# Sums of squares of the query and key heads gathered into 32-row strips, one root and reciprocal for four chunks

## The chip, the cores and the metric

One NeuronCore of a Trainium2 chip runs the whole program. The engines named below are TensorE (PE; PEld is its weight load), VectorE (DVE), ScalarE (ACT), GpSimd (POOL) and SyncE (SP), which here only issues DMAs (transfers between the on-chip memory SBUF and the large memory HBM). Matrix products land in PSUM, eight banks of 128 partitions x 512 fp32 numbers; POOL cannot read PSUM. The metric is the time of one execution on the device in microseconds, the median of several runs.

## The reference

Three layers follow each other on x of shape (4, 1024, 256), all in fp32: half a feed-forward step, an attention step, and half a feed-forward step again.

```python
x = L0_attn_x
x = x + 0.5 * ffn(layernorm(x))
x = x + attn(layernorm(x))
x = x + 0.5 * ffn(layernorm(x))
```

In the attention step, 16 heads of 64 columns each, the part that matters here is the projection and the l2 norm of q and k:

```python
def l2norm(t, eps=1e-12):
    return t / jnp.clip(jnp.linalg.norm(t, axis=-1, keepdims=True), eps)
q = (x @ Wq).reshape(b, n, H, DH).transpose(0, 2, 1, 3)
k = (x @ Wk).reshape(b, n, H, DH).transpose(0, 2, 1, 3)
v = (x @ Wv).reshape(b, n, H, DH).transpose(0, 2, 1, 3)
...
q = l2norm(q)
k = l2norm(k)
dots = jnp.einsum('bhid,bhjd->bhij', q, k) * QK_SCALE
```

After it come a mixing of the heads, a causal mask, the 64 largest scores of each row, a softmax, a second mixing, the product with v, a sigmoid gate and the output projection.

## The kernel before

The program has three stages with a barrier between them: `first_stage` (the first feed-forward layer, and the projections q, k, v and the gates, all stored to HBM), `attention`, and `last_stage`. Only `first_stage` is touched. It loops over M = 8 blocks m of MACRO = 512 tokens.

The order on each engine is written out by hand; the engines meet at semaphores (`s["name"]`), and nothing is rescheduled. For one block TensorE does: `heads(m)`, the 16 chunks c of q and k (128 columns, that is two heads, each), with the values and the turning of the next block's normed x put between; `up(m+1)` and `down(m+1)`, the next block's feed-forward; and `gates(m)`. A chunk has two products of 128x128 by 512 tokens (L314). Head columns lie on the partitions and tokens in the columns, so the sum over a head's 64 columns is a sum over partitions.

A chunk c of q or k goes through these steps before:

- PE L314 makes the chunk in PSUM bank c % 4.
- ACT squares it into `sq` (L431) and copies it to `copy` (L434). These buffers and `rt`, `rr`, `ri`, `qn`, `vo` are parts of tile `a_share` in the profile (copy is `a_copy`).
- PE L323 multiplies `sq` with `blocks` (128x128, 1 where row and column are of one head). Bank 4 + c % 2 then holds the sum of squares of each head, repeated on its 64 partitions.
- ACT takes the root into `rt` (L440), POOL its maximum with 1e-12 into `rr` (L529), DVE the reciprocal into `ri` (L585).
- POOL multiplies `copy` and `ri` into `qn` (L537), and SP stores two chunks at a time (L240).

So root, maximum and reciprocal each work on 128 x 512 numbers per chunk, of which only 2 x 512 differ.

The values (L330), the turned blocks (L277) and the gates (L341) go through banks 6 and 7 in turn, in the order of `side_uses`. In the last block (m = 7) there is no further feed-forward: `early_scores` (L354, L355) makes some scores for the attention between the gates, and DVE takes over the gates' scaling from POOL (`last_gates`, L602). `first_stage` ends when SP has seen the last store land.

Of the kernel before, what the change touches and what calls it, by code (L numbers as in the profile page):

```python
# [25 lines left out]
QC = 2 * HP  # L26
VC = TT * (INNER // 512)
# [32 lines left out]
def build(nc, x, Wq, Wk, Wv, mix_rows, mem_kT, mem_v, hs_col, Wg, bg_col, Wo, WfcT, lnw_col, lnb_col, WpT,  # L60
          ident_c, blocks_c, delta_c, mask_c, guess_c, out):
# [11 lines left out]
    with ExitStack() as top:  # L73
# [7 lines left out]
        with ExitStack() as ctx:  # L81
            ffn_w = ctx.enter_context(nc.sbuf_tensor("ffn_w1", [P, FFN_W], F32))
            first_stage(nc, (banks, ps, ident, ffn_w, eps), x, x1d, Wq, Wk, Wv, Wg, bg_col, hs_col, mem_kT, mkT, qd, kd, vd, gd,
                        wd, ident_c, blocks_c, WfcT, WpT, lnw_col, lnb_col, sd)
# [16 lines left out]
def side_uses():  # L101

    order = []
    for m in range(-1, M):
# [10 lines left out]
        if m >= 0:  # L115
# [4 lines left out]
FIRST_STAGE_SEMS = dict(k0_in=1, q0_in=1, k0=1, s_ps=1, s_sb=1, s_st=1, c_in=6, asum=1, tot=1, wfc=1, tern=1, wp=1, sums=1, done=1, ones=1, kept=1, w_in=7, memk=1, mem=1, x_in=2, link=1, xna=1, xnb=1, side=1, side_out=1, hid=1, gelu=1, sq=1,  # L120
                      stat=1, std=1, hstat=1, hstd=1, gsum=1, out=1, res=1, stored=2, proj=1, raw=1, inv=1, square=1, ssq=1, norm=1,
                      clip=1, qk=1, qk_st=2, v_st=2,
# [3 lines left out]
def first_stage(nc, consts, x, x1d, Wq_d, Wk_d, Wv_d, Wg_d, bg_col, hs_col, mem_kT, mkT, qd, kd, vd, gd, wd, ident_c,  # L126
                blocks_c, WfcT, WpT, lnw_col, lnb_col, sd):
# [4 lines left out]
    with ExitStack() as ctx:  # L132
        def sb(name, shape):
# [26 lines left out]
        copy = sb("copy", [P, 4, MACRO])  # L160
# [4 lines left out]
        blocks = sb("blocks", [P, P])  # L165
        ones = sb("ones", [P, P])
# [15 lines left out]
        sq, rt, rr, ri = [share[:, 2, k * WN // 2:(k + 1) * WN // 2].rearrange("p (k n) -> p k n", k=2)  # L182
                          for k in range(4)]
# [8 lines left out]
        def _(sp):  # L192
# [16 lines left out]
            sp.dma_start(blocks[:], blocks_c).then_inc(s["c_in"][5], 16)  # L209
            sp.dma_start(mraw[:], mem_kT).then_inc(s["w_in"][0], 16)  # L210
# [16 lines left out]
            for m in range(M):  # L227
# [9 lines left out]
                for p in range(HP):  # L237
                    sp.wait_ge(s["qk"], m * QC + 2 * p + 2)
                    c = 2 * p % HP
                    sp.dma_start((qd if 2 * p < HP else kd)[b, :, c:c + 2, tok],  # L240
                                 qn[:, p % 2]).then_inc(s["qk_st"][p % 2], 16)
                    if p == 1 and m + 2 < M:
# [3 lines left out]
                    if p % 2 == 1:  # L246
                        t = p // 2
                        sp.wait_ge(s["side_out"], SIDE["v", m, 2 * t + 1] + 1)
                        sp.dma_start(vd[b, tok][t * P:(t + 1) * P, :], vo[:, t % 2]).then_inc(s["v_st"][t % 2], 16)
# [14 lines left out]
        def _(pe):  # L264
# [15 lines left out]
            def up(m):  # L280
                pe.wait_ge(s["side_out"], SIDE["ta", m, 1] + 1)
                for h in range(FC):
                    if h >= 2:
                        pe.wait_ge(s["gelu"], m * FC + h - 1)
                    elif m >= 1:
                        pe.wait_ge(s["norm"], m * QC - 1 + h)
# [17 lines left out]

            def heads(m):
                pe.wait_ge(s["side_out"], SIDE["tb", m, 1] + 1)
                for c in range(QC + 1):
                    if c < QC:
                        if c >= 4:
                            pe.wait_ge(s["raw"], m * QC + c - 3)  # L310
                        else:
                            pe.wait_ge(s["res"], m * TT + c + 1)
# [4 lines left out]
                    if c >= 1:  # L317
                        pe.wait_ge(s["square"], m * QC + c)
                        if c >= 3:
                            pe.wait_ge(s["norm"], m * QC + c - 2)  # L320
                        else:
                            pe.wait_ge(s["gelu"], (m + 1) * FC)
                        nc.tensor.matmul(ps[4 + (c - 1) % 2][:], blocks[:], sq[:, (c - 1) % 2, :], start=True,  # L323
                                         stop=True).then_inc(s["ssq"], 1)
                    if c < QC and c % 2 == 1:
                        v = c // 2
                        t, h = v // 2, v % 2
                        bank = side_bank(("v", m, v))
                        for k in range(DC):
                            last = nc.tensor.matmul(bank[:], xbT[:, m % 2, k, t * P:(t + 1) * P],  # L330
                                                    W4[:, 2, k, h * 512:(h + 1) * 512], start=(k == 0),
                                                    stop=(k == DC - 1))
                        last.then_inc(s["side"], 1)
                        if v == VC // 2 and m + 1 < M:
                            turn("ta", m + 1)
# [9 lines left out]
            def early_scores():  # L345
# [4 lines left out]
                pe.wait_ge(s["raw"], M * QC)  # L350
                pe.wait_ge(s["norm"], M * QC)
# [36 lines left out]
            for m in range(M):  # L388
# [15 lines left out]
        def _(act):  # L404
# [19 lines left out]

            def heads(m):
                for c in range(QC + 1):
                    if c < QC:
                        act.wait_ge(s["proj"], m * QC + c + 1)
                        if m * QC + c >= 2:
                            act.wait_ge(s["ssq"], m * QC + c - 1)  # L430
                        nc.scalar.activation(sq[:, c % 2, :], ps[c % 4][:], ACT.Square).then_inc(s["square"], 1)  # L431
                        if m * QC + c >= 4:
                            act.wait_ge(s["qk"], m * QC + c - 3)
                        nc.scalar.activation(copy[:, c % 4, :], ps[c % 4][:], ACT.Copy,  # L434
                                             scale=QK_SCALE if c < HP else 1.0).then_inc(s["raw"], 1)
                    if c >= 1:
                        act.wait_ge(s["ssq"], m * QC + c)
                        if m * QC + c >= 3:
                            act.wait_ge(s["clip"], m * QC + c - 2)
                        nc.scalar.activation(rt[:, (c - 1) % 2, :], ps[4 + (c - 1) % 2][:],  # L440
                                             ACT.Sqrt).then_inc(s["norm"], 1)
                    if c < QC and c % 2 == 1:
                        v = c // 2
                        t, h = v // 2, v % 2
                        bank = side_in(("v", m, v))
                        if m * TT + t >= 2:
                            act.wait_ge(s["v_st"][t % 2], 16 * ((m * TT + t) // 2))
                        nc.scalar.activation(vo[:, t % 2, h * 512:(h + 1) * 512], bank[:],
                                             ACT.Copy).then_inc(s["side_out"], 1)
                        if v == VC // 2 and m + 1 < M:  # L450
                            turned("ta", m + 1)
# [51 lines left out]
        def _(pool):  # L503
# [18 lines left out]
            def heads(m):  # L522
                for c in range(QC + 1):
                    i = m * QC + c
                    if c < QC:
                        pool.wait_ge(s["norm"], i + 1)
# [1272 lines left out]
```

## Time and profile before

| What | Value |
|---|---|
| Time, median of 3 runs | 3618.76 us (3610.93 to 3638.0) |
| Time of the profiled execution | 3616.38 us |
| Its span | 3614.0 us |
| Mean granted TensorE clock in it | 0.944 |
| PE busy | 3186.2 us, 88% |
| DVE busy | 2795.0 us, 77% |
| ACT busy | 2567.5 us, 71% |
| POOL busy | 2380.7 us, 66% |
| First stage | 0 to 880.6 us |

The span is what the profiler's records cover; the execution's own time is 2.4 us longer. The busy shares are over all three stages, while the change lies in the first. TensorE does an fp32 product as two records, so a product of the code is two instructions in the profile.

### The profile page before, as it was taken

The page shows a single profiled execution, that of the slowest core. Times are in us where ns is not written, and L with a number is a line of the kernel's source. Part 1 is how long each engine was busy: PE and PEld are TensorE (multiplying, and loading weights), DVE is VectorE, ACT ScalarE, POOL GpSimd, SP SyncE. Part 2 cuts the span into 40 slices and gives each one's busy share as a digit, 9 for nine tenths or more (in the row PEclk, how much of TensorE's full clock was granted, in tenths as well). Part 3 has the DMA queues.
Part 4 walks back from the last instruction along what each step waited for, and adds up shares of the span by engine and source line. Part 5 has one row for each costly group of instructions (what it writes and reads, how often), then busy time and mean ns, then how long its engine had stood idle before and what let it go on. Part 6 is the DMA issues. An engine that isn't in the chain of part 4 may idle for free. (4 is left out here: it accounts for less than half of the span.)

```text
span 3614.0 us, 73990 instructions
## 1 busy us (share of the span) xinstructions
PE 3186.2 (88%) x22950; PEld 2118.9 (59%) x22950; DVE 2795.0 (77%) x6342; ACT 2567.5 (71%) x5953; POOL 2380.7 (66%) x6267
## 2 busy tenths in 40 slices
PE   7999999997788898878999888889988899987898
PEld 4445454443556666755666665566676566666566
DVE  6677766667688999778999867899986888985354
ACT  3444544443688999778899967899986888896221
POOL 2666666655777767688776768776767876674232
PEclk9999999998699999989999998999998999999899
DMA  3223222224456665346666435566534566641110
GB/s 121 99 82 111 105 88 88 82 82 153 135 164 177 187 182 128 90 145 179 178 187 175 100 109 153 170 193 182 152 86 129 168 180 178 180 105 46 38 36 29
DMA packets 363391, 467.04 MB, mean 129 GB/s; under 512 B 29460, under 2 KB 295060, under 8 KB 362520
## 3 DMA queue, kind: packets, MB, share of 16 engines
q1 hardware_dynamic: 362904, 461.54, 43.5%
q8 instruction: 185, 3.03, 0.4%
q14 instruction: 302, 2.47, 0.3%
HBM read 227.09 MB, written 234.36 MB: 128 GB/s over the span
## 5 line engine op out<-in xcount | busy, mean ns | idle before, releaser
L1099 ACT ACTIVATE junk<-D,nt 128x76 int8<-128x76 f32 (+62 forms) x1440 | 1070.2, 747 | 98.4 <-POOL nt L1187 65.5
L1004 PE MATMUL banks<-kr,E 128*128 128x128 f32 (+1 forms) x4672 | 702.9, 299 | 111.1 <-ACT AT L1122 64.6
L1004 PEld LDWEIGHTS banks<-kr,E 128*128 128x128 f32 (+1 forms) x4672 | 602.2, 202 | 258.5 <-issue 154.2
L977 PE MATMUL banks<-Sg,kpre 128*128 128x109 f32 (+51 forms) x1568 | 603.6, 493 | 23.3 <-POOL maskb L1256 13.0
L1329 DVE COPY Sn<-banks 128x686 f32<-128x686 f32 (+11 forms) x440 | 375.9, 854 | 165.7 <-PE banks L964 130.2
L1354 DVE SCALAR_TENSOR_TENSOR W<-SG,sgn,W 128x76 f32<-128x76 int8 (+14 forms) x480 | 413.1, 900 | 104.1 <-POOL W L1209 103.5
L963 PE MATMUL banks<-kT,qT 64*128 64x343 f32 (+11 forms) x880 | 390.3, 525 | 103.6 <-DVE Sn L1329 97.5
L1122 ACT ACTIVATE AT<-banks 128x512 f32<-128x512 f32 (+3 forms) x768 | 344.8, 479 | 185.2 <-PE banks L1004 184.3
L585 DVE RECIPROCAL a_share<-a_share 128x512 f32<-128x512 f32 x128 | 419.9, 3324 | 70.3 <-POOL a_share L529 36.6
L1032 PE MATMUL banks<-AT,V 128*64 128x64 f32 x9216 | 392.8, 233 | 81.9 <-issue 71.5
L1032 PEld LDWEIGHTS banks<-AT,V 128*64 128x64 f32 x9216 | 323.1, 142 | 156.0 <-issue 138.1
L1419 DVE SCALAR_TENSOR_TENSOR E<-D,vk,E 128x12 f32<-128x12 f32 (+56 forms) x512 | 394.5, 779 | 3.1 <-ACT E L1109 1.5
L1099 ACT ACTIVATE SG<-D,nt 128x76 int8<-128x76 f32 (+14 forms) x480 | 357.0, 745 | 50.8 <-DVE hit L1369 48.4
L964 PE MATMUL banks<-kT,qT 64*128 64x343 f32 (+11 forms) x880 | 390.7, 526 | 0.0
L1209 POOL TENSOR_SCALAR W<-D,sgn 128x76 f32<-128x76 f32 (+14 forms) x480 | 376.2, 793 | 0.4
L1109 ACT ACTIVATE E<-D,least 128x12 f32<-128x12 f32 (+56 forms) x512 | 369.3, 721 | 9.6 <-POOL E L1236 6.5
L1340 DVE TENSOR_SCALAR_CACHE_REDUCE D<-banks 128x13 f32<-128x13 f32 (+62 forms) x504 | 339.4, 674 | 40.8 <-PE banks L981 40.3
L977 PEld LDWEIGHTS banks<-Sg,kpre 128*128 128x128 f32 x1568 | 267.0, 205 | 169.3 <-issue 116.2
L1186 POOL TENSOR_TENSOR move<-cnt,tab 128x2 f32<-128x2 f32 x720 | 224.0, 311 | 182.5 <-ACT junk L1099 177.8
L1361 DVE MAX8 m<-W 128x8 f32<-128x76 f32 (+14 forms) x480 | 326.7, 721 | 22.0 <-issue 19.5
L1099 ACT ACTIVATION_READ_ACCUMULATOR junk<-D,nt 128x1 f32 x1440 | 275.4, 191 | 0.0
L529 POOL TENSOR_SCALAR a_share<-a_share 128x512 f32<-128x512 f32 x128 | 190.3, 1487 | 122.0 <-ACT a_share L440 122.0
(195 smaller groups left out, 5710.8 us busy)
## 6 DMA issues: line engine op xcount, KB each, us to landing
score_scratch<-Sn SPq DMA_DIRECT2D x96, 343.0 KB, 3.4
q_scratch<-a_share SPq DMA_DIRECT2D x32, 512.0 KB, 2.7
v_scratch<-a_share SPq DMA_DIRECT2D x32, 512.0 KB, 3.6
k_scratch<-a_share SPq DMA_DIRECT2D x32, 512.0 KB, 2.7
gate_scratch<-a_share SPq DMA_DIRECT2D x32, 512.0 KB, 2.8
kT<-k_scratch SPq DMA_DIRECT2D x32, 512.0 KB, 4.8
gateT<-gate_scratch SPq DMA_DIRECT2D x32, 512.0 KB, 9.8
qT<-q_scratch SPq DMA_DIRECT2D x31, 512.0 KB, 6.4
```

The source lines that it names most:

```text
L585: nc.vector.reciprocal(ri[:, c % 2, :], rr[:, c % 2, :]).then_inc(s["inv"], 1)
L963: nc.tensor.matmul(ps[0][:, 0:c1 - c0], qT[0:DH, p, :], kT[0:DH, p, c0:c1], start=True, stop=True)
L964: nc.tensor.matmul(ps[1][:, 0:c1 - c0], qT[DH:P, p, :], kT[DH:P, p, c0:c1], start=True, stop=True).then_inc(s["s_ps"], 1)
L977: out = nc.tensor.matmul(bank[:, 0:c], kpre[:].rearrange("p h r -> p (h r)"), Sg[:, g % 3, c0:c1], start=True, stop=not diagonal)
L1004: out = nc.tensor.matmul(ps[5 + i % 2][0:rows, c % 4 * P:(c % 4 + 1) * P], E[:, g % 4, c * P:c * P + rows], kr[:, g % 4, :], start=True, s ...
L1032: out = nc.tensor.matmul(into, V[:, c, h * DH:(h + 1) * DH], rows, start=(c == 0), stop=(c == ib and (ib > 0 or hb % 2 == 0)))
L1099: nc.scalar.activation(out, D[:, e, 1:1 + n], ACT.Sign, bias=nt[:, r, e:e + 1], scale=-1.0, accum_out=cnt[:, r, e:e + 1]).then_inc(s[f"cnt ...
L1109: nc.scalar.activation(E[:, g % 4, 0:n], D[:, e, 1:1 + n], ACT.Exp, bias=least[:, e:e + 1], scale=-1.0).then_inc(s["exp"], 1)
L1209: ts(W[:, g % 2, 0:n], D[:, g % 8, 1:1 + n], sgn[:, g % 8:g % 8 + 1], -SMALL, ALU.mult, ALU.mult).then_inc(s["v"], 1)
L1329: nc.vector.tensor_copy(Sn[:, i % 2, :, 0:c1 - c0], banks[:, 0:2, 0:c1 - c0]).then_inc(s["s_sb"], 1)
L1354: nc.vector.scalar_tensor_tensor(out=W[:, h, 0:n], in0=SG[:, h, 0:n], scalar=sgn[:, e:e + 1], in1=W[:, h, 0:n], op0=ALU.is_equal, op1=ALU. ...
L1419: nc.vector.scalar_tensor_tensor(out=E[:, g % 4, 0:n], in0=D[:, g % 8, 1:1 + n], scalar=vk[:, g % 8:g % 8 + 1], in1=E[:, g % 4, 0:n], op0= ...
```

## The change

The norm of q and k is done in GR = 4 groups of four chunks instead of chunk by chunk.

`pick` is a new constant of 128 x 160, loaded by one more DMA in the head of the program. Its first 32 columns map the two heads of a chunk to 32 rows (row r of a strip holds the sum of head r % 2). Its other 128 columns, cut into four strips of 32 rows, map such a strip back to 128 partitions.

```diff
+        pick_c=np.concatenate([p[:, None] // DH == p[None, 0:QG] % 2, p[:, None] % QG == p[None, :] // DH],
+                              axis=1).astype(np.float32),
...
-        copy = sb("copy", [P, 4, MACRO])
+        copy = sb("copy", [P, 8, MACRO])
...
-        sq, rt, rr, ri = [share[:, 2, k * WN // 2:(k + 1) * WN // 2].rearrange("p (k n) -> p k n", k=2)
-                          for k in range(4)]
+        sq = share[:, 2, 0:WN].rearrange("p (k n) -> p k n", k=4)
+        rt, ri = [share[:, 2, k * WN // 2:(k + 1) * WN // 2].rearrange("p (k n) -> p k n", k=2) for k in (2, 3)]
```

On PE, `lengths` makes four products of 128 rows and 32 columns, chunk j of the group to partitions 32j to 32j+31 of one bank. `spread` makes four products of 32 rows and 128 columns, from the same strips of the reciprocals, each to the bank in which chunk j had been:

```diff
+            def lengths(m, g):
+                pe.wait_ge(s["square"], m * QC + 4 * g + 4)
+                if g >= 2:
+                    pe.wait_ge(s["norm"], m * GR + g - 1)
+                else:
+                    pe.wait_ge(s["gelu"], (m + 1) * FC)
+                for j in range(4):
+                    last = nc.tensor.matmul(ps[4 + g % 2][j * QG:(j + 1) * QG, :], pick[:, 0:QG], sq[:, j, :], start=True,
+                                            stop=True)
+                last.then_inc(s["ssq"], 1)
+
+            def spread(m, g):
+                pe.wait_ge(s["inv"], m * GR + g + 1)
+                pe.wait_ge(s["raw"], m * QC + min(4 * g + 8, QC))
+                for j in range(4):
+                    last = nc.tensor.matmul(ps[j][:], pick[j * QG:(j + 1) * QG, QG:QG + P],
+                                            ri[j * QG:(j + 1) * QG, g % 2, :], start=True, stop=True)
+                last.then_inc(s["spread"], 1)
+
             def heads(m):
                 pe.wait_ge(s["side_out"], SIDE["tb", m, 1] + 1)
-                for c in range(QC + 1):
-                    if c < QC:
-                        if c >= 4:
+                for g in range(GR):
+                    for c in range(4 * g, 4 * g + 4):
+                        if g == 0:
+                            pe.wait_ge(s["res"], m * TT + c + 1)
+                        elif g == 1:
                             pe.wait_ge(s["raw"], m * QC + c - 3)
                         else:
-                            pe.wait_ge(s["res"], m * TT + c + 1)
+                            pe.wait_ge(s["qk"], m * QC + c - 7)
...
+                    values(m, 2 * g)
+                    if 2 * g == VC // 2 and m + 1 < M:
+                        turn("ta", m + 1)
...
+                    lengths(m, g)
+                    if g >= 1:
+                        spread(m, g - 1)
+                    values(m, 2 * g + 1)
```

The last group's `spread` stands in the next block's `up`, and in the last block between the gates, with `early_scores` behind it:

```diff
@@ up
+                    if m >= 1 and h == FC - 3:
+                        spread(m - 1, GR - 1)
@@ down
-                        pe.wait_ge(s["raw"], m * QC - TT + t + 1)
+                        pe.wait_ge(s["qk"], m * QC - TT + t + 1)
@@ last block
-                    gates(m, range(2))
+                    gates(m, range(4))
+                    spread(m, GR - 1)
+                    gates(m, range(4, HP - 2))
                     early_scores()
-                    gates(m, range(2, HP - 2))
```

On PE, the second group of a block's heads (four chunks) before (program names: `a_W` the projection weights, `a_xbT` the turned block, `a_share` the squares, `a_blocks` the 128x128 of ones and zeros):

```order
L314 MATMUL banks<-a_xbT,a_W 128x512 x2
L323 MATMUL banks<-a_share,a_blocks 128x512
L314 MATMUL banks<-a_xbT,a_W 128x512 x2
L323 MATMUL banks<-a_share,a_blocks 128x512
L330 MATMUL banks<-a_W,a_xbT 128x512 x2
L314 MATMUL banks<-a_xbT,a_W 128x512 x2
L323 MATMUL banks<-a_share,a_blocks 128x512
```

And PE in the changed kernel, the fourth group of a block and the feed-forward behind it (L351 the chunks, L317 the values, L328 `lengths`, L336 `spread`, L294 `up`, L306 `down`):

```order
L351 MATMUL banks<-a_xbT,a_W 128x512 x8
L317 MATMUL banks<-a_W,a_xbT 128x512 x2
L328 MATMUL banks<-a_share,a_pick 32x512 x4
L336 MATMUL banks<-a_share,a_pick 128x512 x4
L317 MATMUL banks<-a_W,a_xbT 128x512 x2
L294 MATMUL banks<-a_xaT,ffn_w 128x512 x12
L336 MATMUL banks<-a_share,a_pick 128x512 x4
L294 MATMUL banks<-a_xaT,ffn_w 128x512 x4
L306 MATMUL banks<-ffn_w,a_gT 128x257 x32
```

The single sums of squares behind each chunk have moved to one place in a group, a second set of four products has come behind them, and the last set stands behind the sixth of the eight chunks of `up`.

On ACT, a group is four squares and copies, the first value copy, one root, the second value copy. POOL's `heads` is removed as a whole. DVE has a maximum, a reciprocal and four multiplications out of PSUM for each group:

```diff
+            def inverse(m, g):
+                i = m * GR + g
+                dve.wait_ge(s["norm"], i + 1)
+                if i >= 2:
+                    dve.wait_ge(s["spread"], i - 1)
+                nc.vector.tensor_scalar(rt[:, g % 2, :], rt[:, g % 2, :], L2_EPS, None, ALU.max).then_inc(s["clip"], 1)
+                dve.wait_ge(s["clip"], i + 1)
+                nc.vector.reciprocal(ri[:, g % 2, :], rt[:, g % 2, :]).then_inc(s["inv"], 1)
+
+            def normed(m, g):
+                dve.wait_ge(s["spread"], m * GR + g + 1)
+                for j in range(4):
+                    k = m * HP + 2 * g + j // 2
+                    if j % 2 == 0 and k >= 2:
+                        dve.wait_ge(s["qk_st"][k % 2], 16 * (k // 2))
+                    nc.vector.tensor_tensor(qn[:, k % 2, j % 2, :], copy[:, (4 * g + j) % 8, :], ps[j][:],
+                                            ALU.mult).then_inc(s["qk"], 1)
```

DVE in one block before, from the normed x of the next block (L575) to the feed-forward's sums (L610, L616):

```order
L575 TENSOR_SCALAR a_xna<-a_x,a_mv,a_rstd 128x256 x4
L585 RECIPROCAL a_share<-a_share 128x512 x16
L610 TENSOR_TENSOR a_g2T<-a_g2T 128x512 x7
L616 TENSOR_SCALAR a_st<-banks 128x2 x4
```

And the end of the same stretch in the changed kernel (L603 is the multiplication):

```order
L603 TENSOR_TENSOR a_share<-a_copy,banks 128x512 x4
L593 TENSOR_SCALAR a_share<-a_share 128x512
L595 RECIPROCAL a_share<-a_share 128x512
L603 TENSOR_TENSOR a_share<-a_copy,banks 128x512 x4
L636 TENSOR_TENSOR a_g2T<-a_g2T 128x512 x7
```

The reciprocals of a block are four instead of sixteen; the multiplications have come from POOL, each group's behind PE's `spread` of that group and ahead of the next group's maximum.

SP stores the values of a group ahead of the group's q and k pairs, and the load of block m + 2 is issued behind the first values store.

## Rows read from the trace of the kernel before

**Rows 1.** The page, busy time and share of the span of PE and DVE.
```profile
PE 3186.2 (88%) x22950; PEld 2118.9 (59%) x22950; DVE 2795.0 (77%) x6342; ACT 2567.5 (71%) x5953; POOL 2380.7 (66%) x6267
```

**Rows 2.** Windows: two blocks; length, busy PE, PEld, DVE, ACT, POOL, granted clock, DMA.
```profile
591.72:696.90 105.18, 101.55 (x284) 51.47 (x283) 74.82 (x69) 51.41 (x86) 68.09 (x49) 1.00 0.25 90
696.90:801.67 104.77, 101.14 (x280) 51.10 (x279) 73.14 (x61) 50.16 (x85) 66.05 (x49) 0.98 0.23 86
```

**Rows 3.** Waits of PE, 80 to 857 us: total, times, longest.
```profile
PE banks L341 <- ACT a_share L466: 14.4, 7, 2.1
PE banks L298 <- ACT a_gT L423: 4.8, 7, 0.7
```

**Rows 4.** Groups of instructions, 80 to 800 us: busy us, mean ns, idle before.
```profile
L585 DVE RECIPROCAL a_share<-a_share 128x512 f32<-128x512 f32 x111 | 364.3, 3324 | 44.6 <-POOL a_share L529 28.1 <-issue 16.5
L529 POOL TENSOR_SCALAR a_share<-a_share 128x512 f32<-128x512 f32 x110 | 163.6, 1487 | 69.8 <-ACT a_share L440 69.8
L537 POOL TENSOR_TENSOR a_share<-a_copy,a_share 128x512 f32<-128x512 f32 x112 | 142.2, 1270 | 55.2 <-DVE a_share L585 55.2
L323 PE MATMUL banks<-a_share,a_blocks 128*128 128x512 f32 x218 | 111.3, 592 | 0.0
L431 ACT ACTIVATE a_share<-banks 128x512 f32<-128x512 f32 x108 | 64.4, 596 | 102.8 <-PE banks L314 102.8
```

**Rows 5.** Timeline of PE, 803 to 811 us: start, length, count.
```profile
805.10 1.02 PE L323 MATMUL banks<-a_share,a_blocks 128*128 128x512 f32 x2
805.96 1.88 PE L330 MATMUL banks<-a_W,a_xbT 128*128 128x512 f32 x4
807.67 1.88 PE L314 MATMUL banks<-a_xbT,a_W 128*128 128x512 f32 x4
```

**Rows 6.** Timeline of PE at the early scores, products of 64 rows.
```profile
856.60 3.60 PE L341 MATMUL banks<-a_xbT,a_W 128*128 128x512 f32 x8
860.13 0.38 PE L354 MATMUL banks<-a_k,a_q 64*128 64x133 f32 x1
860.13 0.38 PE L355 MATMUL banks<-a_k,a_q 64*128 64x133 f32 x1
860.34 0.27 PE L354 MATMUL banks<-a_k,a_q 64*128 64x133 f32 x1
...
862.15 10.57 PE L341 MATMUL banks<-a_xbT,a_W 128*128 128x512 f32 x24
```

**Rows 7.** Timeline of PE in the attention: products of 64 columns, of 64 rows.
```profile
1304.58 1.62 PE L1032 MATMUL banks<-AT,V 128*64 128x64 f32 x48
1306.13 0.55 PE L963 MATMUL banks<-kT,qT 64*128 64x343 f32 x1
1306.91 0.38 PE L1004 MATMUL banks<-kr,E 128*128 128x128 f32 x1
```

**Rows 8.** DVE: one group by form, two lines with min/median/max ns.
```profile
L1439 DVE TENSOR_TENSOR gateT<-banks,gateT 128x512 f32<-128x512 f32 x43 | 29.4, 685 | 18.5 <-PE banks L1032 18.5
L610 DVE TENSOR_TENSOR a_g2T<-a_g2T x56: 679/1411/1515, 27.8 to 771.6; 128x512 f32<-128x512 f32 x56
L602 DVE TENSOR_SCALAR a_share<-a_share,a_hs x8: 388/478/1496, 863.7 to 875.7; 128x512 f32<-128x512 f32 x8
```

**Rows 9.** Waits for PE, 80 to 857 us.
```profile
ACT a_share L431 <- PE banks L314: 118.9, 118, 1.1
DVE a_st L616 <- PE banks L302: 66.5, 7, 9.5
```

**Rows 10.** Timeline of the first stage's end.
```profile
863.66 2.19 DVE L602 TENSOR_SCALAR a_share<-a_share,a_hs 128x512 f32<-128x512 f32 x3
866.11 0.84 SPq L254 DMA_DIRECT2D gate_scratch<-a_share  x1
876.20 0.51 SPq L254 DMA_DIRECT2D gate_scratch<-a_share  x1
880.61 1.28 ACT L1132 ACT_TABLE_LOAD   x1 [7.17 <-PEq L132]
```

More of the change, by code:

```diff
@@ L26 @@
 QC = 2 * HP
+QG = P // 4
+GR = QC // 4
 VC = TT * (INNER // 512)
@@ L236, in _ @@
                     s["stored"][m % 2], 16)
[L237 to L242, printed above, removed]
+                for g in range(GR + 1):
+                    for p in (2 * g - 2, 2 * g - 1):
+                        if p < 0:
+                            continue
+                        sp.wait_ge(s["qk"], m * QC + 2 * p + 2)
+                        c = 2 * p % HP
+                        sp.dma_start((qd if 2 * p < HP else kd)[b, :, c:c + 2, tok],
+                                     qn[:, p % 2]).then_inc(s["qk_st"][p % 2], 16)
+                    if g < GR:
+                        sp.wait_ge(s["side_out"], SIDE["v", m, 2 * g + 1] + 1)
+                        sp.dma_start(vd[b, tok][g * P:(g + 1) * P, :], vo[:, g % 2]).then_inc(s["v_st"][g % 2], 16)
+                    if g == 0 and m + 2 < M:
                         sp.wait_ge(s["stored"][m % 2], 16 * (m // 2 + 1))
@@ L303, in down, with values @@
                                      start=True, stop=True).then_inc(s["out"], 1)
+            def values(m, v):
+                t, h = v // 2, v % 2
+                bank = side_bank(("v", m, v))
+                for k in range(DC):
+                    last = nc.tensor.matmul(bank[:], xbT[:, m % 2, k, t * P:(t + 1) * P],
+                                            W4[:, 2, k, h * 512:(h + 1) * 512], start=(k == 0), stop=(k == DC - 1))
+                last.then_inc(s["side"], 1)
+            def lengths(m, g):
[15 more added lines that the diff above has]
+                last.then_inc(s["spread"], 1)
             def heads(m):
                 pe.wait_ge(s["side_out"], SIDE["tb", m, 1] + 1)
-                for c in range(QC + 1):
-                    if c < QC:
-                        if c >= 4:
+                for g in range(GR):
[3 more added lines that the diff above has]
+                        elif g == 1:
                             pe.wait_ge(s["raw"], m * QC + c - 3)
                         else:
-                            pe.wait_ge(s["res"], m * TT + c + 1)
+                            pe.wait_ge(s["qk"], m * QC + c - 7)
                         for k in range(DC):
@@ L316, in heads @@
                         last.then_inc(s["proj"], 1)
[L317 to L335, printed above, removed]
+                    values(m, 2 * g)
+                    if 2 * g == VC // 2 and m + 1 < M:
+                        turn("ta", m + 1)
+                    if g == 0 and m == 0:
+                        pe.wait_ge(s["c_in"][6], 16)
+                    lengths(m, g)
+                    if g >= 1:
+                        spread(m, g - 1)
+                    values(m, 2 * g + 1)
             def gates(m, cs):
@@ new lines, in values @@
+            def values(m, v):
+                t, h = v // 2, v % 2
+                bank = side_in(("v", m, v))
+                if m * TT + t >= 2:
+                    act.wait_ge(s["v_st"][t % 2], 16 * ((m * TT + t) // 2))
+                nc.scalar.activation(vo[:, t % 2, h * 512:(h + 1) * 512], bank[:], ACT.Copy).then_inc(s["side_out"], 1)
+            def heads(m):
+                for g in range(GR):
+                    for c in range(4 * g, 4 * g + 4):
+                        i = m * QC + c
+                        act.wait_ge(s["proj"], i + 1)
+                        if c % 4 == 0 and i >= 4:
+                            act.wait_ge(s["ssq"], m * GR + g)
+                        nc.scalar.activation(sq[:, c % 4, :], ps[c % 4][:], ACT.Square).then_inc(s["square"], 1)
+                        if i >= 8:
+                            act.wait_ge(s["qk"], i - 7)
+                        nc.scalar.activation(copy[:, c % 8, :], ps[c % 4][:], ACT.Copy,
+                                             scale=QK_SCALE if c < HP else 1.0).then_inc(s["raw"], 1)
+                    values(m, 2 * g)
+                    if 2 * g == VC // 2 and m + 1 < M:
+                        turned("ta", m + 1)
+                    act.wait_ge(s["ssq"], m * GR + g + 1)
+                    if m * GR + g >= 2:
+                        act.wait_ge(s["inv"], m * GR + g - 1)
+                    nc.scalar.activation(rt[:, g % 2, :], ps[4 + g % 2][:], ACT.Sqrt).then_inc(s["norm"], 1)
+                    values(m, 2 * g + 1)
```

76 lines of the change are left out of this document (15 added, 61 removed).

## The prediction

> **What bounds the kernel now.** I read the page first. PE is busy for 88% of the span [rows 1], but that is a mean over three stages, and the change touches only the first, which ends at 880.6 us [rows 10]. The windows of two of its eight blocks show PE busy for 101.55 of 105.18 us and for 101.14 of 104.77, at a granted clock of 1.00 and 0.98, while DVE has 73 to 75 us, POOL 66 to 68 and ACT 50 to 51 [rows 2]. A busy PE proves little by itself, so I took the waits next. From 80 to 857 us PE waits 14.4 us for a gate's sigmoid and 4.8 us for a gelu, seven times each [rows 3], and some 5 us in smaller sums; none of it is for the norm of q and k. The reader is to see two things. PE's own products set the length of a block, and the chain that the change shortens (root, maximum, reciprocal, multiplication) holds PE up nowhere. The reciprocal at 3324 ns and POOL's 1487 and 1270 ns [rows 4] look costly, but what they give back is worth nothing here. ACT and DVE wait for PE, not the other way: 118.9 us before the squares, 66.5 us before the feed-forward's statistics [rows 9].
>
> So the sum is made of PE's products.
>
> **What goes.** In a block, 16 products with `blocks`. Each costs PE 0.86 us: 805.10 to 805.96, and the next two take 1.71, 0.857 each [rows 5]. The 592 ns of the table [rows 4] is the length of one of a product's two records, which overlap; the step is what counts. 16 x 0.8575 = 13.7 us. On the other engines 16 maxima and 16 multiplications leave POOL (16 x 1.487 + 16 x 1.270 = 44 us), 12 of 16 roots leave ACT and 12 of 16 reciprocals leave DVE (40 us). By the waits above none of this moves the end.
>
> **What comes.** In a block, 16 products of 32 columns and 16 of 32 rows, all with 512 moving columns. A product's price goes by its moving columns, so 32 products one after another are 27.4 us, twice what goes. The question on which everything hangs is whether the four of a set run at once. The trace has no product of 32 rows or columns, so I take the nearest rows.
>
> For rows: the early scores are pairs of 64-row products on both halves of the array, into different banks. Both of a pair start at 860.13, and the stretch from 860.13 to 862.15 holds 16 such pairs of records [rows 6]. A record of 133 columns is 0.8575/2 x 133/512 = 0.111 us; 16 steps are 1.78 us, 32 would be 3.56. It took 2.02. They run at once.
>
> For columns: the values of the attention are products of 64 columns that go to the lower and upper half of one bank in turn. 24 products (48 records) take 1304.58 to 1306.13 [rows 7], 0.065 us each, where 64 moving columns one after another would be 0.8575/8 = 0.107. That is 1.66 at once, in products so short that fixed costs weigh; they too run side by side.
>
> The step from two to four is mine. It has two bounds: a set costs 0.86 us if all four run at once, 1.72 if only two do, and 3.43 if none do. I take 0.86 for both kinds, since both pairs reach nearly their full factor. Eight sets are then 6.9 us.
>
> **The change of shape** has a price of its own, again from rows. Before the early scores PE's products end at 856.60 + 8 x 0.429 = 860.03, and full products start again at 862.15: 2.12 us for 1.78 of steps, 0.34 over. The pair of 343 columns takes 1306.13 to 1306.91, 0.78 us for 2 x 0.287: 0.21 over [rows 6, 7]. I take 0.27 for going to a smaller shape and back. In a block there are four trips with `lengths`, three of them with `spread` right behind (one more change, counted as half a trip), and one trip for the set in `up`: 4 + 1.5 + 1 = 6.5 trips, 1.75 us (1.4 to 2.2).
>
> The Trainium skill has a rule against this change: "TensorEngine Tiling (Array Packing)", Key Properties, says that a change of the tiling mode drains the engine, and gives no price. The 0.21 and 0.34 us of [rows 6, 7] agree that there is one and size it.
>
> The same notes, "TensorE: Matmul & The Clock Gate", Part 3, state 3.07 times for four products of 32 rows and 2.38 for three of 32 columns, at 512 columns. An estimate by that page: 3.43 / 3.07 = 1.12 us a set with its changes in it, 9.0 us a block, which ends at 3582 us; nothing in this trace has sets of four.
>
> **Per block**: 13.7 - 6.9 - 1.75 = 5.1 us less. Eight blocks: 41 us.
>
> **New waits, and what covers them.** PE now waits where it did not:
> - `lengths` needs the square of the group's fourth chunk. ACT squares in 596 ns [rows 4], and the values product ahead of it (two products, 1.72) covers that. Cost 0.
> - `spread` of a group waits for DVE's reciprocal. Between one `spread` and the next PE has six double products and a `lengths`, 6 x 1.715 + 0.96 = 11.2 us. DVE has four multiplications, a maximum and a reciprocal. For the multiplication out of PSUM the row is 685 ns, for the maximum 478 ns [rows 8], the reciprocal 3.3: 2.7 + 0.5 + 3.3 + some 0.5 of handing over = 7.0 us. At the longest that such rows show, 1515 and 1496 ns [rows 8], it is 11.4, level with the cover. Those long ones stand where POOL works beside DVE, and POOL's work on the heads is gone. I take 0.
> - The third group's chunks wait for the multiplications of the first, one by one: 0.69 us each (at worst 1.5) against 1.715 of PE. Cost 0, given the values product ahead of the first.
> - `down` waits for the last group's multiplications. Its `spread` has two chunks of `up` (3.4 us) and a gelu behind it; four multiplications are 2.7. Behind them on DVE are the seven additions of the squares, by L610 up to 1.5 us each: 10.5 us, beside the 13.8 us of `down` (32 products of 257 columns, by columns 0.43 each). The 66.5 us in seven waits [rows 9], 9.5 each, say that DVE came this early; it now comes some 4 us later and still in time. Cost 0.
> - SP issues the same stores in another order, and one small load more at the start. Each stands where its data are ready. Cost 0.
>
> **The end of the stage** is different: not PE sets it but the gates' stores. Before, `last_gates` starts at 863.66, 7.1 us after the heads' last product (856.60), the first gate store is issued at 866.11, the last at 876.20, and the next stage starts at 880.61 [rows 10]. Now DVE must first do the last group's multiplications, behind four gates (6.9) and `spread` (1.0): 8.0 + 2.7 = 10.8 us after the heads, and the first gate store comes at about 11.9 instead of 9.5. The chain of stores shifts by 2.4 us. In return the last block's last `spread` lies in this tail and not in the heads, which the sum above charged with 1.1 us. Together 1.3 us more.
>
> **Sum.** 41 - 1.3 = 39.5 us less. The profiled execution took 3616.38 us, so the forecast is 3577 us. It is 2.4 us under the median of the runs, which themselves spread from 3610.9 to 3638. The price of the shape changes alone gives 3573 to 3580.
>
> **The rivals.**
> 1. *The columns run only two at a time.* For it: four sets of 32 columns read four different streams of 128 rows each, where the trace shows two [rows 7]; the rows' sets read the same amount as one full product. Then `lengths` costs 0.86 us more a group, 3.4 a block, 27 in all: 3604 us.
> 2. *Sets do not run at once as four*: the mechanism by which the change ends slower. A set pays from the point where it is cheaper than (13.7 - 1.75) / 8 = 1.50 us, 1.75 products. With both kinds two at a time it is 1.72 us, and a block gets 1.75 us longer: 14 + 1.3 = 3632 us. With all one after another (3.43) a block gains 13.7 + 1.75 = 15.5 us, and the end is 3741 us. Against it stand the pairs of [rows 6, 7]. Two at a time is the likelier of the two.
> 3. *PE waits for DVE's chain in each group* (multiplications out of PSUM or the maximum run at their slow times). It decides above 11.2 us; each us over costs 24 us in the stage, three groups in eight blocks. 1 us over gives 3601 us. For it: DVE's slow times for the additions (median 1411 [rows 8]). Against it: the multiplication reads only one operand from SBUF, and POOL rests there.
> 4. *The work removed pays as well*: DVE and POOL out of the way let PE's 14.4 us for the gates [rows 3] shrink. That wait hangs on the feed-forward's statistics, which begin at the end of `down` and are unchanged, so at most a few us: 3572.
>
> **How the numbers follow.** Forecast 0.70 (with the fourth rival as its lower end, 3565 to 3588), columns in pairs 0.13 (3604), PE waits for DVE 0.06 (3590 to 3601), sets in pairs 0.07 (3632), one after another 0.04 (3741). The range takes in the first three, 3565 to 3606. About 1% (36 us) is what a measurement of this kernel can tell from no change, and the forecast of 39.5 lies just over it. Faster by over 1%: four fifths of the forecast's 0.70, 0.56. Slower by over 1%: the serial case and a little more, 0.06. Within: 0.38.
>
> **What would show it.** In the changed kernel's timeline, the four products of `lengths` and of `spread` start within some hundredths of a us, and the next full product comes 0.9 to 1.1 us later. A block is 99.7 us instead of 105. PE has no wait for L595 or L603. DVE's reciprocals are 32, and POOL is idle in the heads. The start of the attention lies at 841 us instead of 880.6; the later stages keep their lengths. I am wrong if a set takes 1.5 us or more, if PE waits on DVE inside the heads, or if the granted clock falls in the blocks.

## The result, and the profile after

The changed kernel takes 3580.3 us (median of 4 runs, 3578.9 to 3581.6), the kernel before 3619.2 (median of 4). The ratio is 0.9885, with a 95% interval of 0.9861 to 0.9909: 1.15% faster. The forecast was 3577 us.

The page of the changed kernel, to be set beside [rows 1]:

```profile
span 3576.6 us, 73640 instructions
PE 3147.3 (88%) x23206; PEld 2081.0 (58%) x23206; DVE 2548.2 (71%) x6406; ACT 2522.9 (71%) x5857; POOL 2020.7 (56%) x6011
```

DVE has lost 247 us and POOL 360, but PE 39, and the span 37.4. A block of each kernel in which the granted clock stays at full, from the start of its first chunk to that of the next, the kernel before first (length, busy PE, PEld, DVE, ACT, POOL, clock, DMA share, GB/s):

```profile
172.04:275.96 103.92, 100.29 (x281) 50.90 (x280) 74.83 (x69) 50.78 (x85) 66.88 (x49) 1.00 0.25 91
469.47:568.92 99.45, 95.82 (x314) 46.40 (x312) 44.02 (x77) 45.23 (x73) 21.83 (x17) 1.00 0.25 95
```

The 105.18 us of [rows 2] is no block from chunk to chunk: that window takes in 1.3 us more, and the block inside it is 103.93. DVE has gone from 75 us a block to 44 and POOL from 67 to 22. PE's idle time is what it was, 3.6 us. What PE waits for from 80 to 830 us, to be set beside [rows 3], is also what it was:

```profile
PE banks L368 <- ACT a_share L494: 14.4, 7, 2.1
PE banks L306 <- ACT a_gT L451: 4.8, 7, 0.7
PE banks L294 <- ACT a_gT L451: 2.1, 7, 0.3
```

L368 are the gates, L294 and L306 `up` and `down` of the feed-forward. No line of the new chain (L595, L603) is in the list. The timeline of PE in the last block's third and fourth groups (start, length, count):

```profile
799.87 1.88 PE L317 MATMUL banks<-a_W,a_xbT 128*128 128x512 f32 x4
801.68 1.06 PE L328 MATMUL banks<-a_share,a_pick 128*32 128x512 f32 x8
802.67 1.14 PE L336 MATMUL banks<-a_share,a_pick 32*128 32x512 f32 x8
803.74 1.98 PE L317 MATMUL banks<-a_W,a_xbT 128*128 128x512 f32 x4
805.57 7.03 PE L351 MATMUL banks<-a_xbT,a_W 128*128 128x512 f32 x16
```

L328 is `lengths`, eight records, which one after another would be 8 x 0.429 = 3.43 us; L336 is `spread`, the same. Each is through in about one product's time. Take a values step (L317, four records) at its 1.715 us at either end: from 799.87 + 1.715 = 801.585 to 805.57 - 1.715 = 803.855 the two sets cost 2.27 us, of which 1.715 is two steps of 0.8575 and 0.555 the changes of shape. Where `lengths` stands alone, in the first group of a block:

```profile
575.79 1.88 PE L317 MATMUL banks<-a_W,a_xbT 128*128 128x512 f32 x4
577.60 1.06 PE L328 MATMUL banks<-a_share,a_pick 128*32 128x512 f32 x8
578.59 1.98 PE L317 MATMUL banks<-a_W,a_xbT 128*128 128x512 f32 x4
580.41 7.03 PE L351 MATMUL banks<-a_xbT,a_W 128*128 128x512 f32 x16
```

From 577.505 to 578.695 it costs 1.19 us, 0.33 over one step.

DVE's chain in the last block (L603 the four multiplications, L593 the maximum, L595 the reciprocal), to be set beside [rows 4, 8]:

```profile
816.45 2.48 DVE L603 TENSOR_TENSOR a_share<-a_copy,banks 128x512 f32<-128x512 f32 x4 [6.36 <-PE banks L336]
818.85 0.42 DVE L593 TENSOR_SCALAR a_share<-a_share 128x512 f32<-128x512 f32 x1
819.30 3.35 DVE L595 RECIPROCAL a_share<-a_share 128x512 f32<-128x512 f32 x1
```

The multiplication out of PSUM takes 0.68 us and the whole chain 6.3, and DVE sat idle for 6.4 us before this round. The end of the stage, to be set beside [rows 10]:

```profile
829.60 0.36 SPq L260 DMA_DIRECT2D gate_scratch<-a_share  x1
...
838.57 0.51 SPq L260 DMA_DIRECT2D gate_scratch<-a_share  x1
...
843.35 0.35 SPq L941 DMA_DIRECT2D wrep<-in_mix_rows  x1
```

SPq L941 is the next stage's first load. It stands at 843.35 instead of about 880.6 us, 37.3 us earlier. The two later stages take 3576.6 - 843.35 = 2733.3 us, before 3614.0 - 880.6 = 2733.4. All that the change brings is in the first stage.

**Where the 37.3 us come from.** I read the start of each block's first chunk in both timelines. Blocks in which PE's clock is full throughout last 103.92 us before and 99.45 after, 4.47 less; seven of them make 31.3. Other blocks are 1.1 to 2.4 us longer, with stretches at a lower granted clock in them; summed over seven blocks that is 7.7 us before and 4.6 after, 3.1 less. The first block starts 1.6 us later (68.17 against 66.53), and the last block with the stage's end is 74.4 us instead of 78.9, 4.5 less. 31.3 + 3.1 - 1.6 + 4.5 = 37.3. The first block's start is not the change's doing as far as the runs tell: over all ten traces it lies between 65.8 and 68.2 us, and in experiment seven, with the same code ahead of it, at 66.7.

### The profile page after: what moved, and what is told of

Its sections match the earlier page's. It is cut to its first block and busy times, and to the rows that moved or that the text cites. A ratio compares the mean times of both kernels' runs of the same rounds, so it can differ in the third digit from the quotient of the medians.

```text
span 3576.6 us, 73640 instructions
## 1 busy us (share of the span) xinstructions
PE 3147.3 (88%) x23206; PEld 2081.0 (58%) x23206; DVE 2548.2 (71%) x6406; ACT 2522.9 (71%) x5857; POOL 2020.7 (56%) x6011
## 5 line engine op out<-in xcount | busy, mean ns | idle before, releaser
L537 POOL TENSOR_TENSOR a_g2T<-a_gT 128x512 f32<-128x512 f32 x64 | 73.3, 1150 | 458.5 <-ACT a_gT L451 458.3
L1213 POOL TENSOR_TENSOR nt<-move,base 128x2 f32<-128x2 f32 x720 | 225.2, 313 | 56.4
```

## The experiments

The theory under test: PE's products set the first stage; a set of four small products costs PE about one product plus a change of shape; everything else that the change moves is hidden. The rivals: the sets do not run four at once; the gain comes from the relief of DVE and POOL; the new chain on DVE is as long as its cover. The end of the first stage (the issue of the next stage's first load) is given beside each time, since the later stages vary by themselves (last section).

**One: spread as full products.** The stationary block of each product becomes 128 x 128, with zeros outside the strip's 32 rows.

```diff
-                    last = nc.tensor.matmul(ps[j][:], pick[j * QG:(j + 1) * QG, QG:QG + P],
-                                            ri[j * QG:(j + 1) * QG, g % 2, :], start=True, stop=True)
+                    last = nc.tensor.matmul(ps[j][:], pick[:, 384 + P * j:384 + P * (j + 1)],
+                                            ri[:, g % 2, :], start=True, stop=True)
```

> The changed kernel with each product of 32 rows replaced by a full product: the stationary block is 128x128 with zeros outside the strip's 32 rows, the moving operand all 128 rows. The result is the same numbers. Theory (sets of four run at once, and PE's products set the time): a set of four goes from 0.86 us plus its change of shape to 3.43 us. Beside lengths the two sets now cost 2.27 us of PE together and lengths alone 1.19, so spread with its change costs 1.08 there and becomes 3.43: 2.35 us more in each of 24 groups, and 2.2 more in the eight last ones: about 74 us more than the changed kernel, 3654 us, slower than the kernel before. Rival (the time comes from the relief of DVE and POOL, PE has room): less than 20 us more.

Measured: 3657.5 us (3643.9 to 3662.8), ratio to the kernel before 1.010 (1.007 to 1.014); the stage ends at 919.05, 75.7 us later than in the changed kernel. A block is 108.70 us, 9.25 more. One set in it:

```profile
527.03 1.06 PE L328 MATMUL banks<-a_share,a_pick 128*32 128x512 f32 x8
528.02 3.70 PE L336 MATMUL banks<-a_share,a_pick 128*128 128x512 f32 x8
```

The same eight records take 3.4 us of PE when each fills the array. So the four products of 32 rows do run at once, and PE has no room to hide them: the rival of "less than 20 us" is out.

**Two: lengths as full products**, four that add into one bank.

```diff
-                    last = nc.tensor.matmul(ps[4 + g % 2][j * QG:(j + 1) * QG, :], pick[:, 0:QG], sq[:, j, :], start=True,
-                                            stop=True)
+                    last = nc.tensor.matmul(ps[4 + g % 2][:], pick[:, 256 - QG * j:384 - QG * j], sq[:, j, :],
+                                            start=(j == 0), stop=(j == 3))
```

> The changed kernel with the four products of 32 columns replaced by four full products that add into one bank, each with a stationary block of 128x128 that is zero outside its 32 columns. The result is the same numbers. Theory: 3.43 us for each set instead of 0.86 plus the change of shape: 24 x 2.24 + 8 x 2.24 = 72 us more than the changed kernel, 3652 us. If the 32-column sets in truth ran only two at a time, it would be 24 x 1.4 = 45 us or less. Rival (PE has room): less than 20 us more.

Measured: 3661.3 us (2 runs, 3659.7 and 3662.8), ratio 1.012 (1.006 to 1.017); the stage ends at 919.15, 75.8 us later. A block is 109.01 us, 9.56 more, 2.39 for each set:

```profile
514.53 3.60 PE L328 MATMUL banks<-a_share,a_pick 128*128 128x512 f32 x8
517.97 1.88 PE L317 MATMUL banks<-a_W,a_xbT 128*128 128x512 f32 x4
```

That settles the column sets as well: with pairs only it would have been 45 us or less (32 sets of 1.4 us; the 24 in the text above is a slip).

**Three: both at once.**

> Both replacements at once: no product of a small shape is left, and 32 full products a block stand where 16 were before the change, while root, maximum and reciprocal stay compact. Theory: 13.7 us a block more than the kernel before, eight times, plus or minus the stage's ends: about 110 us over the kernel before, 3729 us. Rival (compact roots and reciprocals carry the gain): near or below the kernel before, 3619 us.

Measured: 3730.8 us (2 runs, 3728.9 and 3732.7), ratio 1.031 (1.025 to 1.037); the stage ends at 993.3, 112.7 us after that of the kernel before. The block with a full clock is 117.66 us: the block before, 103.92, and sixteen products of 0.8575 give 117.64. Compact roots, reciprocals and an idle POOL are all in this kernel, and it is 3% slower than the one before. The relief of the other engines brings nothing by itself.

**Four: the kernel before with a light chain.**

```diff
-                        nc.gpsimd.tensor_scalar(rr[:, c % 2, :], rt[:, c % 2, :], L2_EPS, None,
+                        nc.gpsimd.tensor_scalar(rr[:, c % 2, 0:64], rt[:, c % 2, 0:64], L2_EPS, None,
...
-                    nc.vector.reciprocal(ri[:, c % 2, :], rr[:, c % 2, :]).then_inc(s["inv"], 1)
+                    nc.vector.reciprocal(ri[:, c % 2, 0:64], rr[:, c % 2, 0:64]).then_inc(s["inv"], 1)
```

> The kernel before, with POOL's maximum and DVE's reciprocal of the heads' lengths made on 64 of 512 tokens only; the rest of q and k is not normed rightly, so that part of the computation is left out. PE's work is as before. Theory: nothing on PE waits for this chain, so the time is that of the kernel before within 0.3%, 3610 to 3630 us, though DVE loses some 40 us of work a block. Rival (the gain of the change comes from the reciprocals): 30 us or more faster than the kernel before.

Measured: 9813 us. As a time this is a miss, and it says nothing on the question. The two later stages took 8929 us instead of 2733: with lengths that are wrong the attention fell into its general search for each row's 64 largest scores (L1390, 3744 instructions here, none in the trace of the kernel before). I had not thought of that. Its first stage does not depend on the numbers and can be read. A window over one block, and the start of the next stage:

```profile
280.78:384.72 103.94, 100.31 (x282) 50.89 (x281) 26.75 (x69) 50.79 (x85) 46.87 (x49) 1.00 0.29 101
```
```profile
883.01 0.35 SPq L915 DMA_DIRECT2D wrep<-in_mix_rows  x1
```

DVE has 27 us of work in a block instead of 74, and the block is 103.94 us, as before. The stage ends at 883.0 us, 2.4 later than in the kernel before and not earlier. With PE's work unchanged, a lighter chain gains nothing.

**Five and six: a longer chain on DVE**, one and three reciprocals more in each group, ahead of the one that PE waits for:

```diff
+                for e in range(1):
+                    nc.vector.reciprocal(spare[:, e, :], rt[:, g % 2, :])
                 nc.vector.reciprocal(ri[:, g % 2, :], rt[:, g % 2, :]).then_inc(s["inv"], 1)
```

> The changed kernel with one more reciprocal of 128x512 (3.35 us, into a spare buffer) in each group's chain on DVE, ahead of the one that PE waits for. In the changed kernel's trace the group's reciprocal ends some 5 us ahead of the spread that needs it. Theory (the cover holds): no wait of PE for L597 or its like, the first stage ends where the changed kernel's does, 843 us, within 2 us; total 3580 us. Rival (the chain is as long as its cover): PE waits in each group and the stage is 24 x 3.35 = 80 us longer.

> Three more reciprocals in each group's chain, 10.05 us. The cover of some 5.1 us is used up by the first one and a half, so each of the three later groups of a block makes PE wait about 4.9 us: 24 x 4.9 = 118 us more, the first stage ends near 961 us and the total is near 3698 us. Rival (PE's order hides more than that): less than 40 us more.

Measured with one more: 3571.9 us (2 runs, within 0.8 us), the stage ends at 842.5, and five of its seven blocks are 99.44 to 99.46 us. The cover holds at 3.35 us more, but for one wait: in the last block, where only four gates stand ahead of the last `spread`, PE waits 0.8 us for it, and that block with the stage's end takes 76.0 us instead of 74.4. With three more: 3725.9 us (3713.4 and 3738.4), ratio 1.030 (1.025 to 1.034), the stage ends at 978.9, 135.5 us later than in the changed kernel, where 118 were expected. PE's waits, 80 to 960 us, show the chain at last:

```profile
PE banks L337 <- DVE a_share L598: 90.6, 32, 6.0
```

All 32 sets wait, not the 24 that I had counted, and by 2.8 us each on average, not 4.9. The timeline of PE around two of them:

```profile
457.91 2.09 PE L337 MATMUL banks<-a_share,a_pick 32*128 32x512 f32 x8 [3.13 <-DVE a_share L598]
459.93 3.75 PE L318 MATMUL banks<-a_W,a_xbT 128*128 128x512 f32 x4
463.50 7.05 PE L352 MATMUL banks<-a_xbT,a_W 128*128 128x512 f32 x16
470.39 1.88 PE L318 MATMUL banks<-a_W,a_xbT 128*128 128x512 f32 x4
472.20 1.07 PE L329 MATMUL banks<-a_share,a_pick 128*32 128x512 f32 x8
475.96 1.14 PE L337 MATMUL banks<-a_share,a_pick 32*128 32x512 f32 x8 [2.70 <-DVE a_share L598]
```

Eight records last 2.09 us instead of 1.14, and four 3.75 instead of 1.98: in the window from 457.91 to 463.50 the granted clock is 0.50, its level of 1.2 GHz, right after PE had waited for 3.13 us. What such a stretch costs depends on where it falls. In a block of the changed kernel the four `spread` sets stand 13.9, 12.6 and 13.9 us apart (490.64, 504.54, 517.11, 530.96), here 17.1, 18.1 and 17.1 (440.81, 457.91, 475.96, 493.07): DVE's longer chain sets the distance, and PE waits at 475.96 again. So the slow records behind the set are hidden in the next wait, and only the set's own 0.95 us comes on top.

The 17 us beyond the expected 118 are these. A block is 16.1 us longer on average, where 3 x 4.9 = 14.7 were expected: the set in `up` waits too (1.0 to 1.7 us), and some slow stretches fall on a set or behind the last one. The last block with the stage's end is 23.8 us longer, also against 14.7; its last `spread` has only four gates as its cover and waits 6.0 us. The first block starts 0.9 us earlier: 7 x 16.1 + 23.8 - 0.9 = 135.6 (rounded terms).

**Seven: the two sets of a group apart**, `spread` ahead of the second values product and `lengths` behind it (and ACT's root behind the second value copy).

```diff
-                    lengths(m, g)
                     if g >= 1:
                         spread(m, g - 1)
                     values(m, 2 * g + 1)
+                    lengths(m, g)
```

> The changed kernel with spread ahead of the second values product and lengths behind it, so that the two sets of small shapes in a group no longer touch. Theory (each change of shape costs PE): 24 groups have two trips of 0.33 us instead of one joined trip of 0.56 us: 0.10 us a group, 0.3 us a block, 2.5 us in all; the block of 99.45 us becomes 99.8. Rival (the price is in each set itself, not in the change): 99.45. The time itself is too coarse to tell.

Measured: 3582.3 us (3578.5 and 3586.1), not to be told from the changed kernel; the stage ends at 849.5, 6.1 us later, of which eight blocks at 0.60 us are 4.8. Blocks with a full clock are 100.04 to 100.07 us, 0.60 more than 99.45: 0.20 for each of the three groups whose sets were parted, where I had 0.10 (0.33 + 0.37 - 0.555 = 0.15 with the lone sets as they measured, see below). PE's timeline:

```profile
492.51 1.14 PE L336 MATMUL banks<-a_share,a_pick 32*128 32x512 f32 x8
493.58 1.98 PE L317 MATMUL banks<-a_W,a_xbT 128*128 128x512 f32 x4
495.49 1.07 PE L328 MATMUL banks<-a_share,a_pick 128*32 128x512 f32 x8
```

From 493.58 to 495.49 two full products between two sets take 1.91 us, not 1.715. The price is in the change of shape, and sets of different shapes are best put side by side.

**Eight: PE's own waits trimmed.** If PE sets the stage, its waits are the next thing to take.

```diff
@@ ACT, block loop
-                gates(m, range(3))
+                gates(m, range(4))
                 if m + 1 < M:
                     spread("tb", m + 1)
-                gates(m, range(3, HP - 2))
+                gates(m, range(4, HP - 2))
@@ PE, down
-                pe.wait_ge(s["gelu"], (m + 1) * FC)
                 for t in range(TT):
...
                     for h in range(FC):
+                        if t == 0:
+                            pe.wait_ge(s["gelu"], m * FC + h + 1)
@@ PE, last block
-                    gates(m, range(4))
+                    gates(m, range(3))
                     spread(m, GR - 1)
-                    gates(m, range(4, HP - 2))
+                    gates(m, range(3, HP - 2))
```

> The changed kernel with three waits of PE trimmed: ACT does four gates ahead of the next block's root instead of three; down waits for each gelu as its first row tile reaches it instead of for all eight; in the last block spread stands behind three gates instead of four. Theory (PE sets the first stage, so only PE's own waits are left to take): of 2.06 us at the gates about 1 us goes, 0.7 us at down goes, seven times, and 1.7 us at the end: 11 to 14 us off, 3567 us. Rival (another engine is the bound of a block by now): no change, 3580 us.

Measured: 3565.2 us (4 runs, 3562.9 to 3567.9), ratio to the kernel before 0.9852 (0.9832 to 0.9872), 15 us under the changed kernel's median. It is the fastest of all. Its waits of PE, 80 to 815 us:

```profile
PE banks L283 <- ACT a_share L495: 7.3, 7, 1.0
PE banks L294 <- ACT a_gT L452: 2.1, 7, 0.3
PE banks L283 <- ACT a_share L459: 1.8, 7, 0.3
PE banks L369 <- ACT a_xbT L443: 1.2, 7, 0.2
```

The waits for gelu in `down` are gone. The one at the gates has moved to the turned block behind them (L283) and is halved: 14.4 and 1.7 us have become 7.3. A block is 97.26 us, 2.2 less than 99.45, and six of the seven are alike within 0.01: the stretches at a lower clock have gone with the waits of 2 us. The stage ends at 823.9 us, 19.4 earlier; 2.3 of that is a first block that starts earlier (65.83 against 68.17), and the later stages in this run take 6.8 us more. The third edit brought nothing: the last block with the stage's end takes 74.95 us, against 74.41 in the changed kernel. Its first gate store comes sooner (9.8 us behind the heads instead of 11.5), but the early scores begin where they did, 11.66 us behind the heads, DVE later waits 3.8 us for a gate store to land instead of 2.3, and the last store comes 0.7 us later. Why that store lands later stays open. The three edits ran together; the blocks tell the first two from the third.

## Why the prediction was right

**PE bounds the stage.** Shown: full products in place of the small ones cost what their time on PE is (experiments one to three), and a light chain on DVE and POOL leaves the block at 103.94 us (four).

**A set of four costs one step.** This was the open step, from two at once in the trace to four, and it held for rows and columns both: 1.19 us with the change of shape for the columns alone, 2.27 for both, where serial sets take 3.43 each. The first rival (columns in pairs, 3604 us) and the second (sets in pairs, or serial) are out by these rows.

**The change of shape was mis-sized.** The term was 6.5 trips of 0.27 us, 1.75 us a block, bounds 1.4 to 2.2. Measured are 0.33 for `lengths` alone and 0.555 for each of three joined trips. For the set in `up`, experiment one gives it: of its 9.25 us a block three groups take 3 x (1.19 + 3.43 - 2.27) = 7.05, which leaves 2.20 for replacing the lone `spread`, so that costs 3.43 - 2.20 = 1.23, 0.37 over a step (a value by difference, good to some 0.05 us). The sum is 0.33 + 1.67 + 0.37 = 2.4 us a block, above my upper bound. Two things were small: the single trip, for which the row of 0.34 us was the right one and the 0.21 not, and the change from one small shape to the other, which costs 0.2 (if each change to or from full is half its trip) and not 0.135. By the measured terms a block saves 13.72 - 6.86 - 2.37 = 4.49 us; the blocks show 4.47. The Trainium skill's rule in "TensorEngine Tiling (Array Packing)", Key Properties, that a change of the tiling mode drains the engine, agrees in that each change costs PE time. Here the changes, 2.4 us, take back a third of the 6.9 us a block that the packing saves.

**The estimate by the Trainium skill** ("TensorE: Matmul & The Clock Gate", Part 3), 1.12 us a set, was nearer than my own terms: it gives 8.9 us a block for the eight sets where I had 8.6, and measured are 9.2 (lone sets cost 1.19 and 1.23, joined ones 1.13 each). Its time was summed wrongly: 8 x (13.72 - 8.94) - 1.3 is 37 us less, 3579 and not 3582. The 3.07 times that this page of the Trainium skill states for four products of 32 rows stands beside 3.43 / 1.23 = 2.8 here, for fp32 at 512 columns.

**The hidden edits stayed hidden.** No wait of PE for the squares, the reciprocal or the multiplications is in the list. The multiplication took 0.68 us, as the row out of PSUM had it, not the 1.5 us of the additions between SBUF operands. Those additions themselves (L610, now L636) have fallen from a median of 1411 ns to 693 now that POOL does less, which no PE wait rewards. The chain of 6.3 us against a cover of 11.5 has 5 us to spare, which experiments five and six bracket: one reciprocal more is free, three are not. The third rival is out.

**The end of the stage** was put at 1.3 us more, net. The last block's heads save 5.7 us (6.2 in the prediction, the difference again the change of shape), and behind them the end takes 25.2 us instead of 24.0, 1.2 more where I had 2.4. The first gate store came 11.5 us behind the heads, where I had 11.9, but the chain of stores after it was shorter, and the last one came only 0.8 us later than before.

**Not in the sum**: 3.1 us of lower clock that seven blocks lost before and do not lose now, and a first block 1.6 us later. Neither is explained by the change. The fourth rival had PE's wait at the gates shrink; it is 14.4 us in both.

So 39.5 us was forecast and 37.3 is what the stage shows. Seven blocks at 4.47 instead of 5.1 us make 4.5 less, the last block with the end 0.7 more than its 3.8, and the two terms outside the sum 1.5 more: -4.5 + 0.7 + 1.5 = -2.3 (rounded). The mechanism is the predicted one; that the total lies within 2.3 us is partly luck, since the shape term alone was off by twice that. By medians the kernels differ by 38.9, and the four runs of the kernel before lie 27 us apart.

## What to carry to other kernels

- Four fp32 products of 32 rows or 32 columns in different strips of the array cost TensorE about one full product (0.86 us at 512 columns) and 0.3 to 0.4 us for the change of shape. So where a product uses a quarter of the array, gather four into a set, and put sets of different shapes next to each other.
- Compaction that relieved only engines that wait was worth nothing in time here. Ask what TensorE does per block, and count steps from start to start.
- When TensorE bounds a stage, a wait of 2 us on it can cost another 1.1 to 1.7 us at half clock. Taking such waits out (eight: 15 us) paid over a third of what the whole change did, with a few moved lines.

## What the hardware showed that I had not expected

**Stretches at half clock behind a wait.** In the kernel before, after one 2.05 us wait of PE at the gates, four records last 3.58 us instead of 1.98:

```profile
373.11 3.58 PE L341 MATMUL banks<-a_xbT,a_W 128*128 128x512 f32 x4 [2.05 <-ACT a_share L466]
```

and the window over them has a granted clock of 0.53:

```profile
373.11:376.48 3.37, 3.37 (x4) 1.21 (x5) 1.29 (x8) 0.52 (x1) 3.10 (x2) 0.53 0.26 100
```

The same wait of 2.05 us at 689.29 us has no such stretch behind it:

```profile
689.29 1.99 PE L341 MATMUL banks<-a_xbT,a_W 128*128 128x512 f32 x4 [2.05 <-ACT a_share L466]
```

Blocks of one kernel differ by 1.1 to 1.7 us for it; the first block, which follows a wait of 10 us, has such a stretch at its start in both kernels and is 1.6 and 2.4 us longer. In experiment eight, where the longest wait at the gates is 1.0 us, six blocks in a row are without one. What decides whether a given wait is followed by it, no run here tells.

**The later stages vary by themselves.** From the end of the first stage to the end of the span the unchanged code took 2733.4 us before and 2733.3 in the changed kernel, but 2725.4 in experiment one, 2727.5 in five, 2738.2 in two and 2740.0 in eight. That is 15 us, 0.4%, and as much as experiment eight's gain. Each of these is one execution of one kernel, so whether the kernel or the execution makes the difference is not shown; the five executions of experiment one alone lie 19 us apart. For a change in one stage the end of that stage, read from the trace, is the sharper measure.
